# Self attention with nine score steps per two heads instead of twelve, TensorE's pieces put in another order, and row maxima transposed from 72 columns

## What is computed

```python
q, k, v = (split_heads(x @ W) for W in (Wq, Wk, Wv))      # 2 x 16 heads, 1024 x 64
q, k = apply_rope(q), apply_rope(k)
sim = einsum('bid,bjd->bij', q, k) * 64 ** -0.5            # where j <= i, -inf elsewhere
out = einsum('bij,bjd->bid', softmax(sim), v)
x = layernorm(x + merge_heads(out) @ Wo + bo)
```

## Time and profile before

| | us |
|---|---|
| median of 3 runs | 957.85 (957.36 to 958.19) |
| profiled execution, its time | 955.91 |
| profiled execution, its span | 954.1 |
| PE busy | 862.2 (90%) |
| DVE busy | 702.7 (74%) |
| POOL busy | 660.6 (69%) |
| ACT busy | 455.1 (48%) |
| chain that ended last | PE 71%, DVE 11%, POOL 8%, issue 6% |

### The profile page before, as it was taken

How to read it: one execution, slowest core, us unless ns; L and a number is a source line. 1 busy time by engine, 2 the same in 40 slices (tenths; PEclk the granted TensorE clock), 3 DMA queues, 4 the chain that set the end, 5 groups by cost and what they waited for, 6 DMA issues and landing times.

```text
span 954.1 us, 17785 instructions
## 1 busy us (share of the span) xinstructions
PE 862.2 (90%) x6312; PEld 626.8 (66%) x6312; DVE 702.7 (74%) x1697; ACT 455.1 (48%) x1101; POOL 660.6 (69%) x638
## 2 busy tenths in 40 slices
PE   3778999999999999999999999999989988787854
PEld 2554666666656666666666666677679888776744
DVE  3679888687787876997868768553469789788762
ACT  2323545445455354454554544656666555434240
POOL 2567797797887878989879788755846223535793
PEclk9888999999999999999999999999999999789987
DMA  8000200000000000000000000323201001110111
GB/s 259 23 12 2 61 23 7 18 13 18 15 5 29 12 7 29 2 18 24 7 18 1 14 29 1 103 86 97 66 12 55 12 24 45 45 34 23 56 50 49
DMA packets 33192, 33.49 MB, mean 35 GB/s; under 512 B 3600, under 2 KB 27984, under 8 KB 33104
## 3 DMA queue, kind: packets, MB, share of 16 engines
q1 hardware_dynamic: 32336, 30.26, 10.5%
q0 software_dynamic: 768, 2.10, 0.7%
HBM read 24.45 MB, written 7.77 MB: 34 GB/s over the span
## 4 chain that ended last, share of the span: by engine, by line
PE 71%; DVE 11%; POOL 8%; issue 6%; ACT 3%; DMA 1%; SPq 1%; DVEq 0%; ACTq 0%; POOLq 0%
PE bank L546 30%; PE bank L617 15%; PE bank L637 13%; PE bank L586 5%; PE bank L551 3%; POOL SUM L442 2%; PE bank L649 1%; ACT W_f L967 1%; DVE X L1170 1%; POOL REG L1361 1%; PE bank L763 1%; POOL rs L1409 1%; PE bank L622 1%; DVE st L1155 1%; DVE W_f L1274 1%
## 5 line engine op out<-in xcount | busy, mean ns | idle before, releaser
L442 POOL TENSOR_TENSOR SUM<-SUM,PT_f 128x512 f32<-128x512 f32 (+3 forms) x272 | 254.0, 953 | 28.4 <-PE bank L637 20.7
L862 ACT ACTIVATE PT_f<-bank 128x512 f32<-128x512 f32 (+3 forms) x320 | 132.8, 467 | 188.1 <-PE bank L622 121.8
L617 PE MATMUL bank<-REG 64*128 64x512 f32 (+3 forms) x1152 | 152.8, 362 | 5.2 <-DMA MR<-MH 3.9
L1096 DVE CUSTOM_DVE_ANT_0 bank<-bank,later 128x128 f32<-128x128 f32 (+3 forms) x256 | 118.5, 521 | 40.7 <-PE bank L586 40.7
L617 PEld LDWEIGHTS bank<-REG 64*128 64x128 f32 x1152 | 98.6, 186 | 51.1 <-issue 35.5
L637 PE MATMUL bank<-PT_f,VV_f 128*64 128x512 f32 (+3 forms) x640 | 118.2, 482 | 0.0
L546 PE MATMUL bank<-XH,W_r 128*128 128x512 f32 x256 | 96.8, 422 | 20.6 <-POOL W_r L1361 18.8
L1386 POOL TENSOR_TENSOR RW_f<-RW_f,sinS 128x512 f32<-128x512 f32 x64 | 82.3, 1287 | 42.0 <-DVE RW_f L1068 41.6
L1361 POOL TENSOR_TENSOR W_r<-W_f,W_r 128x512 fp32r<-128x512 f32 (+1 forms) x56 | 66.0, 1183 | 56.5 <-ACT W_r L812 56.4
L1361 POOL TENSOR_TENSOR REG<-RW_f,REG 128x512 fp32r<-128x512 f32 x64 | 87.6, 1370 | 11.8 <-ACT REG L812 11.8
L1099 DVE TENSOR_REDUCE NM<-bank 128x1 f32<-128x512 f32 x128 | 80.8, 682 | 12.3 <-PE bank L586 12.3
(11 more groups left out here) (196 smaller groups left out, 2037.2 us busy)
## 6 DMA issues: line engine op xcount, KB each, us to landing
W_f<-in_cw SPq DMA_DIRECT2D x16, 256.0 KB, 2.8
W_f<-in_Wq SPq DMA_DIRECT2D x16, 128.0 KB, 2.5
W_f<-in_Wk SPq DMA_DIRECT2D x16, 128.0 KB, 2.6
XR_f<-in_xT SPq DMA_DIRECT2D x8, 256.0 KB, 3.8
W_f<-in_Wv SPq DMA_DIRECT2D x8, 256.0 KB, 3.3
W_f<-in_Wo SPq DMA_DIRECT2D x16, 128.0 KB, 2.3
...
```

The source lines that it names most:

```text
L442: e.e.tensor_tensor(s, s, p_at(n, par)[:, 0:512 - o0], ALU.add).then_inc({"g": g_sum, "v": v_sum}[on], 1)
L617: i = e.matmul(ST[par][:, 0:w], keys[rows, :], qs[rows, q0:q0 + w], start=k == 0, stop=k == 3 and not diag)
L862: e.activation(p_at(n, par)[:, 0:w], ST[par][:, 0:w], ACT.Exp, scale=D ** -0.5).then_inc(a_exp, 1)
L1096: e.tensor_tensor_reduce(s, s, later[:, 512 - w:512], -1.0, -NEG, ALU.add, ALU.min, NM[gp % 2][:, col:col + 1]).then_inc(v_mr, 1)
```

## The change

There are four edits, all in the self attention.

1. **Nine steps.** `SIDES` packs the twelve tiles in nine steps whose columns sum to 512: (0,1) with (0,3), (0,2) with (1,6), and (1,5) with (1,7), written as (c, kt). The other six steps hold one full tile each. The matmuls are the same in number and width. ACT takes 18 exponentials of 512 columns for a pair instead of 24 of four widths. `pv` comes in four pieces of 4, 3, 2 and 3 tiles (`PVS`) instead of six of two. The adds are chained in the order of `CHAIN`; DVE has (1,1), (1,3), (1,5) of one head instead of (1,2), (1,4), (1,6).
2. **Order.** `PAIR` is new: `mx` now runs for up to two pairs ahead (g0 to g8 between 7.78 and 15.95, counted from the start of pair gp - 2), and pieces that use the array in the same way stand next to one another more often. `FIRST` is a table of its own for pair 0, for the pair that loads the second half of x, and for the layer norm of the first batch entry, whose four parts go to pairs 9 to 12 instead of the end of pair 8.
3. **Maxima from 72 columns.** `NM` is 88 wide; the maxima of c = 0 stand in columns 0 to 7, those of c = 1 in 72 to 79, with zeros between. `turn` transposes 72 columns (0 to 71 or 8 to 79), and `put` takes rows 0 to 7 or 64 to 71 of the result.
4. Small moves in `ENDS`, `TAIL` and `FFN`, with counts of semaphores to match.

```diff
-STEPS = 12 * NSELF
+SC = 9
+STEPS = SC * NSELF
-PAIR = {"g0": 0.02, "pv": 0.43, "p0": 1, "p1": 1.01, "v0": 1.02, "su": 1.04, "sm": 1.2, "a0": 1.41, "g1": 1.44,
...
+PAIR = {"os": 0.02, "w3": 0.03, "p0": 0.04, "p1": 0.16, "sm": 1.75, "a0": 1.8, "l0": 2.08, "a1": 2.17, "v0": 2.35,
...
-ADDS = {(c, kt, par): "v" if (kt, par) in ((2, 0), (4, 0), (6, 0)) and c else "g"
-        for c, kt in TILES if kt for par in range(2)}
+SIDES = [[(0, 0)], [(0, 1), (0, 3)], [(0, 2), (1, 6)], [(1, 0)], [(1, 1)], [(1, 2)], [(1, 3)], [(1, 4)],
+         [(1, 5), (1, 7)]]
+PVS = [[(0, 0), (0, 1), (0, 3), (0, 2)], [(1, 0), (1, 6), (1, 1)], [(1, 2), (1, 3)], [(1, 4), (1, 5), (1, 7)]]
+CHAIN = [t for piece in PVS for t in piece if t[1]]
+ADDS = {(c, kt, par): "v" if (kt, par) in ((1, 0), (3, 0), (5, 0)) and c else "g" for c, kt in CHAIN for par in range(2)}
+RING = [s for s in range(SC) if s not in (0, 3)]
...
-        if gp == NP:
-            items += [(9.9 + 0.25 * k, ev) for k, ev in enumerate(ln_pieces(0))]
+        if NP < gp <= NP + 4:
+            items += [(FIRST["ls"], ("lns", gp - NP - 1)), (FIRST["lr"], ("lnr", gp - NP - 1))]
...
-        NM = [sb(f"NM{i}", [128, 24]) for i in range(2)]
+        NM = [sb(f"NM{i}", [128, 88]) for i in range(2)]
-        MH = [sb(f"MH{i}", [8, 128], R) for i in range(2)]
+        MH = [sb(f"MH{i}", [72, 128], R)[64 * i:64 * i + 8, :] for i in range(2)]
...
-                e.transpose(bk[0:8, 0:128], NM[gp % 2][:, 8 * c:8 * c + 8], idF[:, :]).then_inc(p_nt, 1)
+                pe.wait_ge(v_pad, 2)
+                e.transpose(bk[0:72, 0:128], NM[gp % 2][:, 8 * c:8 * c + 72], idF[:, :]).then_inc(p_nt, 1)
...
+                for c, kt in SIDES[s]:
+                    o, w = WHERE[c, kt][1], tile_width(c, kt)
+                    q0 = 512 * c + 512 - w
...
+                            i = e.matmul(ST[par][:, o:o + w], keys[rows, :], qs[rows, q0:q0 + w], start=k == 0,
+                                         stop=k == 3 and not diag)
...
-                    e.activation(p_at(n, par)[:, 0:w], ST[par][:, 0:w], ACT.Exp, scale=D ** -0.5).then_inc(a_exp, 1)
+                    e.activation(o[:, :], ST[par][:, :], ACT.Exp, scale=D ** -0.5).then_inc(a_exp, 1)
...
+            for m in NM:
+                e.memset(m[:, 8:72], 0.0).then_inc(v_pad, 1)
```

More of the change, by code:

```diff
@@ L116, in plan @@
         ("vp", 0, 3), ("qs", 1))
-    carried = [(0.1 + 0.45 * j, ("mx", 0, 3 + j)) for j in range(6)]
-    carried += [(2.8, ("least", 0)), (2.9, ("turn", 0, 1)), (3.2, ("put", 0, 1))]
+    at = FIRST
+    carried = [(at[f"m{3 + j}"], ("mx", 0, 3 + j)) for j in range(6)]
+    carried += [(at["least"], ("least", 0)), (at["turn1"], ("turn", 0, 1)), (at["put1"], ("put", 0, 1))]
     for n in range(4):
-        carried += [(0.6 + 0.7 * n, ("pj", 1, n)), (1.0 + 0.7 * n, ("ad", 1, n)), (1.2 + 0.7 * n, ("st", 1, n))]
+        carried += [(at[f"p{n}"], ("pj", 1, n)), (at[f"a{n}"], ("ad", 1, n)), (at[f"l{n}"], ("st", 1, n))]
     for gp in range(NSELF):
@@ L126, in at @@
         def at(key):
[L127 removed]
+            return 3.0 + PAIR[key] * 0.66 if gp == 0 else PAIR[key]
         if gp + 2 < NSELF:
@@ L418, in op_at, with p_at @@
             return REG[:, o:o + 1024]
-        def p_at(n, par):
-            gp, c, kt = step_of(n)
-            return PT[order_of(n) % 4][par] if kt else SUM[2 if c else gp % 2][par]
+        def p_at(gp, c, kt, par):
+            s, o = WHERE[c, kt]
+            b = PT[order_of(gp, s) % 4][par] if kt else SUM[2 if c else gp % 2][par]
+            return b[:, o:o + tile_width(c, kt)]
         def added(e, gp, c, kt, par):
@@ L605, in scores @@
-                w = 512 * c + 512 - q0
-                diag = kt >= 4 * c
-                ks = slice(128 * kt, 128 * kt + 128)
-                ready(pe, gp, c, kt // 4)
                 pe.wait_ge(v_aug, 3)
                 mr = MR[:, 1024 * (gp % 2):1024 * (gp % 2) + 1024]
-                terms = [(op_at(gp, 2)[:, ks], op_at(gp, 0)), (op_at(gp, 2)[:, ks], op_at(gp, 1)),
-                         (op_at(gp, 3)[:, ks], op_at(gp, 0)), (oneR[:, :], mr)]
-                for k, (keys, qs) in enumerate(terms):
-                    for par, rows in enumerate(HEAD):
-                        if k == 0 and n:
-                            pe.wait_ge(a_exp, 2 * n + par - 1)
-                        i = e.matmul(ST[par][:, 0:w], keys[rows, :], qs[rows, q0:q0 + w], start=k == 0,
-                                     stop=k == 3 and not diag)
@@ L636, in p_v @@
                     for par, rows in enumerate(HEAD):
[L637 to L639 removed]
+                        i = e.matmul(OB[rows, 512 - tile_width(c, kt):512],
+                                     VV[vb][:, kt, col + 64 * par:col + 64 * par + 64], p_at(gp, c, kt, par),
+                                     start=kt == 0, stop=(c, kt) in ((0, 2), (1, 7)))
```

182 lines of the change are left out of this document (101 added, 81 removed), and 29 rows, old and new, of tables (FFN, FIRST, PAIR, TAIL).

## The result

Four runs of the changed kernel gave a median of 943.5 us (939.99 to 944.64) against 958.0 (957.36 to 958.91) before: a ratio of 0.984, interval 0.981 to 0.987. That is faster by 14.5 us where 27 were forecast; it lies at the upper edge of the range. The profiled execution took 944.1 us, its span is 942.0 and its mean granted clock 0.952 (before 955.9, 954.1 and 0.959).

The account below looks back on a forecast made before the run. PE's work and its order were taken to bound pairs 1 to 13. Gains of 20.2 + 2.4 + 2.5 + 2 = 27.1 us took the profiled 955.9 to 928.8, for the median 930.8; range 922 to 944.

Parts of the forecast that it names:

- The steady pair: Pairs 1 to 13: fewer switches of array use shorten each from 38.19 to 36.64 us, 20.2 us in all.
- taken as rows to columns: Price assumed for PE's switch from 64 rows to the sums, which no row showed; bounds 0.04 and 0.20 us.
- The transpose of 72 columns: Maxima transposes in each pair: counted as full-array work of 0.10 us, with no switch beside full-array work.
- Rival 3: The new maxima transpose stays its own array use or costs a switch: 5 to 6 us missing, 936 us; chance 0.08.
- Waits that go: Extra length of pairs 5 and 9, 3.5 us over steady: 2.5 us taken as gained, bounds 0 and 3.5.
- Rival 4: Maxima of c = 1 arrive late by DMA in each of 14 pairs, 6.7 us each: 1025 us; chance 0.05.
- Rival 2: All switches of array use cost alike, 0.19 us, so a pair saves 2.1 us: 923 us; chance 0.07.
- Rival 1: Another engine becomes the bound, one place a pair late by 0.8 us, giving back 12 us: 943 us; chance 0.20.
- Pair 0: First pair: MR lands about 4 us earlier; 2 us taken as gained, bounds 6 gained and 3 lost.
- 2 for small waits: Allowance in the first pair for PE's waits after MR lands, beside 31.4 us of work and 2.5 for low clock.
- Pairs 14 and 15: Last two pairs, with cross attention's heads: 17 fewer switches at mean 0.14 gain 2.4 us; bound 0 if chain is late.
- The rest: Tail after the last pairs, where `TAIL` and `FFN` move single pieces: 0 us, bounds 2 either way.

Follow-up runs that it names:

- `apart`: The changed kernel with four entries of PAIR moved, putting three switches of array use back without added work: 954.83 us in one run, steady pair 37.65 us.
- `turn8`: The changed kernel with the maxima transposed from 8 columns again instead of 72: median 938.65 us, steady pair 36.65 us.
- `hold_kt`: The changed kernel with unread dummy matmuls filling TensorE's two longest waits before the heads' context matmuls in pairs 14 and 15: median 938.86 us, ratio 0.980.
- the second execution: A second profiled execution of the changed kernel, unaltered, from a rerun of five: 937.86 us, span 936.0; the rerun's median was 939.67 us.

## Why the prediction was right or wrong

*The steady pair.* Right: 36.69 for 36.64, PE busy in all of it, full clock. The sums between uses of rows take 0.42 from the last `mx` (214.55 to 214.97) where four 256-column matmuls have 0.24 by the prices, so "taken as rows to columns", 0.18 to 0.19, was the right end of the open price. The `pv` of four tiles takes 2.31 (221.03 to 223.34). `apart` shows that the gain is in the order.

*The transpose of 72 columns.* The number is right and the reading wrong. The sum took the new one as full-array work, which it is; but so was the old one. The fit had given it a use of its own with 0.10 out, since before it always stood ahead of rows, and that 0.10 was the switch to rows. Rival 3 was priced on this misreading: `turn8` costs nothing, so it could not have come true.

*Waits that go.* Pair 9 is at 36.73, the steady length, as said. Pair 5 is at 38.09, 1.40 over it (2.06 before), and pair 6 at 37.89, 1.20 over; 1.31 and 1.00 of these are two new waits for DVE's maxima. So the two pairs together have more extra than before (2.6 for 2.1), 1.4 us of the 2.5 taken as gained is missing, and the steady pairs, 1.50 shorter instead of 1.55, miss 0.7. That is 2.1 in pairs 1 to 13, within the bound named.

*Rival 4* fell as argued: no wait on MR in pairs 1 to 13. *Rival 2* fell: the measured prices of rows and columns differ by a factor of three. *Rival 1* did not come as told: POOL and DVE made no wait in each pair, so the steady pairs lost nothing. Its number, 943, is what was measured, and this is luck: what came is a late chain and a lower clock in two pairs of sixteen. The range holds the result by 0.5 us, and only because it took in rival 1 up to that size.

*Pair 0.* Wrong step: "2 for small waits". The wait on MR came as forecast (3.11 us, clock 0.88 in the pair), but beside it stand 3.59, 1.96 and three of 2.8 together for DVE. I had laid DVE's rows in order up to the arrival of MR and not beyond it, though DVE was busy for 47.6 of 57.3 us; it is 50.8 of 56.6 now. So pair 0 is 0.8 us shorter and not 2. And the sum had no term for the stretch ahead of it: the first score matmul comes at 40.07 instead of 38.32, 1.75 later. Why is open; in `hold_kt`, whose queue is the same up to there, it comes at 39.37, and pair 0 takes 58.7.

*Pairs 14 and 15.* This is the step that failed, 11.5 us between -2.4 and +9.1. Its two halves: the count of switches times a mean price, 2.4, of which the sum of work shows nothing (100.2 before, 100.7 in `hold_kt`, at full clock in both); and the bound "0, if the chain from DMA over ACT and POOL to the heads is late", which allowed for lost gain but not for loss. The chain was late by 2.5 us more than before, in waits of 1.2 to 2.3, and the clock fell for 6.1 more in the first profile (three times, once behind the wait of 0.31) and some 3 in the second (twice). I had worked out just this cost for the wait of pair 0 and not carried it to the end.

The first half was not wrong in its count: the trace has 17 changes of array use fewer in this stretch, as said (71 and 54, for 68 and 51). But the new order also puts work into it, which the sum left out. The stretch begins with a `pv` of three tiles carried over from pair 13 where it was two, and the last sums are cut in two around a wait for POOL. Before (first group) and in `hold_kt`:

```profile
598.00 0.87 PE L637 MATMUL bank<-PT_f,VV_f 128*64 128x256 f32 x8
694.09 1.07 PE L649 MATMUL bank<-SUM,ones 128*32 128x512 f32 x8
```

```profile
579.93 1.94 PE L686 MATMUL bank<-PT_f,VV_f 128*64 128x512 f32 x12
676.80 1.05 PE L698 MATMUL bank<-SUM,ones 128*32 128x512 f32 x4
679.09 1.46 PE L698 MATMUL bank<-SUM,ones 128*32 128x512 f32 x4 [1.24 <-POOL SUM L486]
```

To the next matmul the `pv` takes 0.80 before and 1.87 now, the sums 0.99 and, without the wait, 2.44. That is 2.5 us more, where the work grew by 0.5. So some 2 us of the 2.4 may well be there, an estimate from these rows; no run tests it.

*The rest.* -1.6 and -4.2 in two profiles of one kernel, so the bound of 2 either way was too narrow: with the same queue for this stretch, runs took 247.7 to 252.3.

With the second execution in the place of the first, the sum is 18.1 off 954.1 where 27.1 was forecast; 8.4 of the missing 9.0 are pairs 14 and 15. The other three misses, 2.6 and 2.2 us short and 4.2 over, nearly cancel.
